# The expert stage computed on sorted tokens instead of on all tokens

## The reference

```
logits = xf @ gate_w.T                                # xf: 2048 x 256, rms-normalised
topk_vals, topk_idx = top_k(logits, 2)
topk_gates = softmax(topk_vals)
gates = zeros((2048, 8)); gates[row, topk_idx] = topk_gates
h = silu(einsum('nd,ehd->neh', xf, exp_w1))           # every expert on every token
eo = einsum('neh,edh->ned', h, exp_w2)
sel = einsum('ned,ne->nd', eo, gates)                 # six of the eight gates of a token are zero
out = x + silu(xf @ sh_w1.T) @ sh_w2.T + sel
```

## Time and profile before

| | |
|---|---|
| time, median of 3 runs | 3418.31 us (3410.98 to 3420.01) |
| profiled execution, first to last instruction | 3419.0 us |
| TensorE matmul busy | 3026.8 us (89%) |
| VectorE, ScalarE, GpSimd busy | 56%, 44%, 13% |
| mean granted TensorE clock | 0.930 |
| DMA, mean over the span | 48 GB/s |
| expert stage, from its first instruction to the first of the next stage | 1457.6 to 2316.4 us |

### The profile page before, as it was taken

One profiled execution on the slowest core, in us unless ns is written; L12 is line 12 of the kernel. 1 busy time (PEld: TensorE's weight loads), 2 busy tenths in 40 slices (PEclk: granted clock), 3 DMA queues, 4 the chain that ended last, 5 costly groups with the idle time before them and its releaser, 6 DMA issues. The chain is left out here.

```text
span 3419.0 us, 47618 instructions
## 1 busy us (share of the span) xinstructions
PE 3026.8 (89%) x17126; PEld 1808.1 (53%) x17248; DVE 1914.5 (56%) x4677; ACT 1492.1 (44%) x2134; POOL 451.8 (13%) x538
## 2 busy tenths in 40 slices
PE   6888888856999999989999999996999999978686
PEld 3444333342444444379898989993444444347353
DVE  4666777654767776443333333334777777734354
ACT  1333444521555555544444444431555555543233
POOL 0111111143211111010000000001122221113112
PEclk7889888976999999989999999997999999998798
DMA  4212121103222222000000000003222222100331
GB/s 116 49 40 57 46 64 46 30 1 70 76 61 82 67 77 60 18 25 26 26 25 26 26 26 26 1 1 69 78 61 87 58 76 58 30 1 1 83 86 49
DMA packets 75113, 162.66 MB, mean 48 GB/s; under 512 B 15401, under 2 KB 21673, under 8 KB 72697
## 3 DMA queue, kind: packets, MB, share of 16 engines
q1 hardware_dynamic: 74872, 159.51, 17.8%
HBM read 60.76 MB, written 2.10 MB: 18 GB/s over the span
## 5 line engine op out<-in xcount | busy, mean ns | idle before, releaser
L883 ACT ACTIVATE probT_a<-scores 128x1024 f32<-128x1024 f32 (+3 forms) x832 | 785.1, 949 | 841.8 <-PE scores L737 469.8
L992 DVE CUSTOM_DVE_ANT_0 ring<-ring,maskb_a 128x512 f32<-128x512 f32 x1024 | 681.9, 719 | 204.8 <-PE ring L754 175.1
L754 PE MATMUL ring<-stacks_a 64*128 64x512 f32 (+7 forms) x1664 | 451.9, 422 | 72.2 <-DMA stacks_a<-fixed_a 26.0
L1329 DVE TENSOR_TENSOR hidden_moe<-whole_moe,hidden_moe 128x512 fp32r<-128x512 f32 x288 | 199.8, 694 | 519.9 <-ACT whole_moe L1251 519.7
L775 PE MATMUL outputs<-probT_a,V_a 128*32 128x512 f32 (+6 forms) x3328 | 451.1, 586 | 23.9 <-ACT probT_a L883 11.8
L1172 PE MATMUL scores<-tokens_moe,weights_moe 128*128 128x512 f32 x1728 | 447.8, 395 | 4.9 <-issue 4.9
L719 PE MATMUL scores<-stacks_a 64*128 64x512 f32 (+7 forms) x1664 | 415.6, 480 | 0.0
L719 PEld LDWEIGHTS scores<-stacks_a 64*128 64x128 f32 (+1 forms) x1664 | 166.4, 188 | 464.0 <-issue 344.9
L990 DVE TENSOR_REDUCE negm_a<-ring 128x1 f32<-128x512 f32 (+3 forms) x640 | 329.7, 562 | 144.5 <-PE ring L760 103.2
L1185 PE MATMUL ring<-weights_moe,hidden_moe 128*128 128x256 f32 x2592 | 402.8, 283 | 4.0 <-DVE hidden_moe L1329 3.4
L1185 PEld LDWEIGHTS ring<-weights_moe,hidden_moe 128*128 128x128 f32 x2592 | 367.6, 191 | 30.7 <-issue 4.6
(11 more groups left out here) (151 smaller groups left out, 3240.7 us busy)
## 6 DMA issues: line engine op xcount, KB each, us to landing
stacks_a<-parts_a SPq DMA_DIRECT2D x672, 128.0 KB
raw<-in_moew SPq DMA_DIRECT2D x9, 2048.0 KB, 7.5
maski_a<-in_mask SPq DMA_DIRECT2D x16, 1024.0 KB, 5.3
wt<-in_w SPq DMA_DIRECT2D x7, 1024.0 KB, 5.0
kvT_a<-in_ctxT SPq DMA_DIRECT2D x12, 512.0 KB, 3.5
stacks_a<-fixed_a SPq DMA_DIRECT2D x4, 1024.0 KB
wrow<-in_row SPq DMA_DIRECT2D x7, 512.0 KB, 6.2
stacks_a<-mrow_a SPq DMA_DIRECT2D x224, 8.0 KB
```

The source lines that it names most:

```text
L754: last = pe.matmul(bank("S", j, n, e)[:, 0:w], Q[rows, g, qt * P:(qt + 1) * P], K[rows, g, 0:w], start=True, stop=not a.causal)
L883: act.activation(probT[:, kb % 2, 2 * p:2 * p + 2, q0:S], scores_bank(j, n)[:, :, q0:S], ACT.Exp, bias=0.0, scale=-1.0).then_inc(c_exp.sem, 1)
L992: least = dve.tensor_tensor_reduce(sc, sc, maskb[:, m % 2, qt, :], 1.0, BIG * 2, ALU.add, ALU.min, out)
L1329: dve.tensor_tensor(hidden[:, m % 4, 1, :], whole[:, m % 2, :], hidden[:, m % 4, 0, :].bitcast(F32), ALU.subtract).then_inc(c_low.sem, 1)
```

## The change

The eight experts are no longer computed on all tokens; the shared one still is. `feed_block` serves f0 and f2 alone; a new `routed_block` lays out the expert stage.

- The beginning of the stage is as before, but the normalised tokens are also stored to a DRAM tensor `moe_tokens`, and four copies of `xs` exist instead of two.
- The shared expert comes first, 32 steps as before. Beside them the routing is worked out: ranks of the (token, expert) pairs within their expert by 17 float32 matmuls with a triangle and with ones (step 6), the extent of each expert in tiles of 256 slots (steps 7 and 8), the slot of each pair, and by 32 float32 matmuls with one-hot matrices (steps 15 to 22) the token and the gate of each slot (`addresses`, step 23).
- Then come 23 tiles of 256 slots, the number that suffices whatever the draw; all 23 are always computed. A tile is 4 steps. A step is 12 matmuls of 256 columns (two slices of the hidden width over 256 slots), the same two Silu of 512 columns, the same subtraction, and 12 matmuls of 256 columns of the second layer.
- Each tile loads its expert's 2 MB in four quarters by SyncE, whose address comes from a value computed on chip; ScalarE and VectorE split one quarter (1024 columns) in each step.
- GpSimd gathers a tile's 2 x 128 rows by two indirect DMAs; TensorE turns them with 4 transposes, ScalarE and VectorE split them. The outputs are scaled by the gate on ScalarE (256 columns, twice) and added by two indirect DMAs with accumulation into a DRAM tensor `moe_total`, each pair after the pair before it has landed.
- After the last tile SyncE reads `moe_total` back in four pieces and VectorE adds them to X.
- At the start of the program GpSimd zeroes `raw`, and SyncE writes it to `moe_total` (2 MB and 256 KB), ahead of the copies into `stacks`.
- The first-layer results use three PSUM banks in turn instead of four; the fourth serves the routing and the turned rows.

```diff
+SL = 2 * P
+TILES = (2 * NT * P + E * (SL - 1)) // SL
...
+                sp.wait_ge(m_zero, 1)
+                sp.dma_start(total[0:NT * P, :].rearrange("(p n) d -> p (n d)", p=P), raw[:, :]).then_inc(m_cleared, 16)
+                sp.dma_start(total[NT * P:(NT + 2) * P, :].rearrange("(p n) d -> p (n d)", p=P), raw[:, 0:2 * D])                    .then_inc(m_cleared, 16)
...
+            for i in range(TILES):
+                e = sp.value_load(expert_i[0:1, i:i + 1], min_val=0, max_val=E)
+                for c in range(4):
+                    sp.wait_ge(m_wlow, 4 * i + c + 1)
+                    sp.dma_start(raw[:, quarter(c)], io["moew"][bass.ds(e, 1), :, quarter(c)]
+                                 .rearrange("o p n -> (o p) n")).then_inc(m_raw[c], 16)
+            sp.wait_ge(m_scatter, 32 * TILES)
+            for b in range(B):
+                sp.dma_start(xs(b), total[b * QT * P:(b + 1) * QT * P, :].rearrange("(q p) d -> p q d", p=P))\
+                    .then_inc(m_sum[b], 16)
...
+            def gather(i):
+                for j in range(2):
+                    pool.indirect_dma_start(
+                        out=gathered(i, j), out_offset=None, in_=spread_rows[:, :],
+                        in_offset=bass.IndirectOffsetOnAxis(ap=row_from[:, 2 * i + j:2 * i + j + 1], axis=0))\
+                        .then_inc(m_gather[i % 2], 16)
+            def scatter(i):
+                pool.wait_ge(m_scaled, i + 1)
+                if i == 0:
+                    pool.wait_ge(m_cleared, 32)
+                else:
+                    pool.wait_ge(m_scatter, 32 * i)
+                for j in range(2):
+                    pool.indirect_dma_start(
+                        out=total[:, :], in_=scaled(i, j), in_offset=None, compute_op=ALU.add,
+                        out_offset=bass.IndirectOffsetOnAxis(ap=row_to[:, 2 * i + j:2 * i + j + 1], axis=0))\
+                        .then_inc(m_scatter, 16)
+            gather(0)
+            gather(1)
+            for i in range(TILES):
+                if i + 2 < TILES:
+                    pool.wait_ge(m_rows, i + 1)
+                    gather(i + 2)
+                if i >= 1:
+                    scatter(i - 1)
+            scatter(TILES - 1)
...
+            for s in range(STEPS + 2):          # TensorE
+                i, q = step(s)
+                if s < STEPS:
+                    first_layer(s)
+                nxt, at = divmod(s - SHARED + 4, 4)
+                if at == ROWS_AT and 0 <= nxt < TILES:
+                    turn_rows(nxt)
+                if s >= 2:
+                    second_layer(s - 2)
+                if s == RANK_AT:
+                    ranks()
+                if INVERSE_AT <= s < INVERSE_AT + 8:
+                    inverses(s - INVERSE_AT)
...
+            for s in range(STEPS):              # ScalarE
+                act.wait_ge(m_hid, s + 1)
+                if s >= 2:
+                    act.wait_ge(m_low, s - 1)
+                for dst in (hidden[:, s % 4, 0, :], whole[:, s % 2, :]):
+                    last = act.activation(dst, RING[s % 3], ACT.Silu)
+                last.then_inc(m_high, 1)
+                nxt, at = divmod(s - SHARED + 4, 4)
+                if 0 <= nxt < TILES:
+                    whigh(nxt, at)
+                    if at == ROWS_AT:
+                        act.wait_ge(m_rows, nxt + 1)
+                        for kb in range(KB):
+                            act.activation(rowsT[:, nxt % 2, 0, kb, :], TURN[:, kb * SL:(kb + 1) * SL], ACT.Identity,
+                                           bias=0.0, scale=norm3[:, kb:kb + 1]).then_inc(m_rowhigh, 1)
+                if at == 2 and 2 <= nxt:
+                    scale_out(nxt - 2)
```

More of the change, by code:

```diff
@@ L1117, in chunk @@
         def chunk(q):
             return slice(q * S, (q + 1) * S)
-        SPLIT = {6 + 3 * q: q for q in range(f.chunks)} if moe else {}
-        def landed(it, more):
-            before = {"f0": 0, "moe": 1, "f2": 1 + FEED["moe"].experts}[st]
-            return it * (16 * PER_TURN) + 16 * (before + more + 1)
-        @block.sync
-        def _(sp):
-            if moe:
-                with sp.Fori(0, TURNS) as it:
-                    for n in range(PER_TURN):
-                        sp.wait_ge(c_wlow.sem, c_wlow.at(st, it, (n + 1) * f.chunks))
-                        load_expert(sp, st, it * PER_TURN + (n + 1))
+        landed = 16 if st == "f0" else 48
@@ L1235, in _ @@
         @block.scalar
         def _(act):
-            def split(it, slot, q, done):
-                if q == 0:
-                    act.wait_ge(c_raw, landed(it, done))
-                act.activation(weights[:, slot, 0, chunk(q)], raw[:, chunk(q)], ACT.Copy).then_inc(c_whigh.sem, 1)
-            def turn(it, experts):
-                for m in range(experts * f.blocks):
-                    slot, n, at = m // f.blocks, m % f.hb, m % f.blocks
-                    act.wait_ge(c_hid.sem, c_hid.at(st, it, m + 1))
-                    act.wait_ge(c_low.sem, c_low.at(st, it, max(m - 1, 0)))
-                    for dst in (hidden[:, m % 4, 0, :], whole[:, m % 2, :]):
-                        if moe:
-                            last = act.activation(dst, RING[m % 4], ACT.Silu)
-                        else:
-                            last = act.activation(dst, RING[m % 4], ACT.Relu, bias=wcolf[:, n:n + 1], scale=1.0)
-                    last.then_inc(c_high.sem, 1)
-                    if experts > 1 and at in SPLIT:
-                        split(it, 1 - slot, SPLIT[at], slot + 1)
@@ L1266, in _ @@
                 b, kb = j // KB, j % KB
[L1267 to L1272 removed]
+                if j == 0:
+                    act.wait_ge(c_raw, landed)
@@ L1282, in _ @@
-            if moe:
-                act.wait_ge(c_gex, 1)
-                act.activation(gex[:, 1, :], gex[:, 0, :], ACT.Exp).then_inc(c_gate, 1)
-                with act.Fori(0, TURNS) as it:
-                    turn(it, PER_TURN)
-                turn(TURNS, 1)
-            else:
-                turn(0, 1)
+                act.activation(tokens[:, 0, kb, b * S:(b + 1) * S], RING[j % 4], ACT.Copy).then_inc(c_thigh.sem, 1)
+            for m in range(f.blocks):
+                n = m % f.hb
+                act.wait_ge(c_hid.sem, c_hid.at(st, 0, m + 1))
+                act.wait_ge(c_low.sem, c_low.at(st, 0, max(m - 1, 0)))
+                for dst in (hidden[:, m % 4, 0, :], whole[:, m % 2, :]):
+                    last = act.activation(dst, RING[m % 4], ACT.Relu, bias=wcolf[:, n:n + 1], scale=1.0)
+                last.then_inc(c_high.sem, 1)
```

758 lines of the change are left out of this document (544 added, 214 removed).

## The result

The changed kernel takes 2997.3 us (median of 4 runs, 2989.05 to 3005.43) against 3418.1 us before: ratio 0.8779 (95% interval 0.8757 to 0.88). The forecast was 2995. (3418.1 is the median of four runs; the table ahead has the first three.) The profiled execution has a span of 2995.0 us against 3419.0.

A forecast was written before the change was run, and what follows sets the result against it. TensorE, bound by columns, was taken to set the pace; the expert stage falls from 859 to 426.5 us (29.5 + 381 + 16), so 3419.0 - 432.5 + 8 = 2994.5, forecast 2995 us, range 2965 to 3085.

The forecast's parts named there:

- TensorE's pace: In the tiles: TensorE bound by columns, 2.86 us a step, 11.9 us a tile with the turned rows; 62% as forecast.
- the turning: In each tile: 4 transposes of the gathered rows on TensorE, 0.5 us a tile, 11.5 us in all.
- Main part: Expert stage between beginning and end: shared expert 90.2, tiles 263.1, turning 11.5, routing 14, fill and drain 2: 381 us.
- the routing matmuls: Beside the shared expert: 17 + 32 float32 matmuls, 98 records on TensorE, 12 to 22 us, taken as 14.
- ScalarE 85%, VectorE 8.5 us a tile: In the tiles: ScalarE 10.1 us, 85% of a tile, and VectorE 8.5 us, both hidden behind TensorE's 11.9.
- 1.5 us an indirect DMA: GpSimd's two gathers and two scatters in each tile: 1.5 us apiece, 6 us a tile, hidden.
- Rival C: In the tiles: GpSimd blocks VectorE's subtractions, a tile 13.1 us, 28 us more, 3023 us; 17% with late weights and slow ScalarE.
- the beginning stays 29.5: Expert stage before its main part: stays 29.5 us, from 1457.6 to 1487.01.
- The row of 1.84 us: Profile row used for rival C: a two-operand SBUF subtraction took 1.84 us beside a GpSimd operation, 0.69 alone.
- The end: After the last second-layer matmul: scaling, scatters, landing, read-back and addition uncovered, 17.4 us, taken as 16; bounds 11 to 28.
- The program start: Before the first stack copy: two issues and 2.25 MB of writes add 8 us, bounds 1 to 12.
- The range of A: Whole kernel if TensorE sets the tiles' pace: 2975 to 3015 us, from routing, start and tail; chance 62%.

The follow-up runs named there:

- the two kernels with the quarter behind the tiles: Changed kernel with the shared expert's last quarter computed after the tiles: alone 2986.6 us; with later clears and 512-column pieces in the beginning too, 2979.2 us.
- the fastest version: Changed kernel with clears moved to the first attention stage, 512-column pieces in the beginning, and the shared expert's last quarter after the tiles: 2979.2 us.

## Why the prediction was right, point by point

- **TensorE's pace.** Steps of 2.87 us (2.86 forecast), the turning 0.44 (0.5), a tile 11.95 (11.9). Two tiles fewer took 23.9 us off TensorE's part; ScalarE's margin was shown by doubling its rounding, GpSimd's by doubling the indirect DMAs, the weights' by undoing the quarters. Main part: 381.3 us (1499.15 to 1880.46) for 381. That it fits to 0.3 us is luck: the routing matmuls were 3.7 + 6.5 = 10.2 us instead of 14 and the turning 1.4 us less in all, and the first blocks at the low clock (18 first-layer matmuls take 6.38 us here, 5.83 in the earlier trace rows), two waits for VectorE's additions (0.90 and 1.62 us) and 0.01 us on each of the steps made up for it.
- **ScalarE 85%, VectorE 8.5 us a tile:** 80% = 9.6 us, and 70% = 8.4 us. ScalarE's margin was larger than priced, mostly by a slip in the sum: the earlier trace rows gave 1.20 - 0.21 = 0.99 us for a Silu pair, and I took 1.1, 0.4 us a tile.
- **GpSimd.** 1.5 us an indirect DMA was the middle: 0.94 for a quiet gather, 1.55 for a scatter, 0.1 to 1.1 us more when held, plus 0.3 between them. A tile occupies the queue for 8.3 us against 6 forecast; hidden both ways.
- **Rival C** asked the right question about the wrong side. In the tiles no subtraction exceeded 1.23 us; it was GpSimd that was held. It did happen in the beginning: the argument "the beginning stays 29.5" overlooked that subtractions of 1024 columns meet GpSimd's normalisation for longer than those of 512. It became 31.4 us (+2.0). The row of 1.84 us was rightly read; what was wrong is the step from it to the tiles, where an indirect DMA is held and doesn't hold.
- **The end:** 17.9 us; my terms added to 17.4 and I had shaved that to 16 because the scatters' halves would overlap. They didn't: 1.55 + 0.3 + 1.55, then the landing. The 17.4 came that near by compensation: the landing took 2.2 us instead of 4, and from the read-back's issue to the next stage 10.9 instead of 9.5.
- **The program start:** +5.1 instead of +8. The writes cost 4.1 us of waiting, not 7: most of the 2.25 MB ran beside loads, slowly.
- **The whole.** The expert stage lost 428.3 us instead of 432.5: beginning 1.9, main part 0.3 and end 1.9 us longer than forecast, 4 in all. The start was 2.9 us cheaper, and the other stages, which the sum left alone, came out 0.6 us shorter in this profile: 1.6 longer to a2 beyond the start, a2 and a3 3.5 longer, a4 to f2 5.2 and a6 0.5 shorter. 2994.5 + 4.0 - 2.9 - 0.6 = 2995.0. So the mechanism and the stage's price to 1% are the forecast's merit, the 0.1% of the whole is luck. The differences outside belong to no step: they lie within what executions of the same code differ by, that from a4 to f2 only if the two kernels with the quarter behind the tiles are counted.
- **The range of A** was added up too narrow: its three terms give 2981 to 3019, not 2975 to 3015. Nothing hung on it.

## What to carry to other kernels

Where one engine is bound by columns and the trace has a start-to-start time per column, a rewritten stage can be priced closely (here a tile at 11.9 us that takes 11.95); spend the remaining effort on the two ends of the stage, where nothing is hidden, and on every duration whose partner engine changes. Indirect DMAs of 128 rows cost their engine 0.9 to 2.5 us each here and are free as long as their sum with the gaps stays under the tile. A weight buffer refilled in pieces as it is consumed needs no second copy; refilled whole it costs the wait and then the clock.

## What was not expected of the hardware

- An indirect DMA on GpSimd is delayed by the remainder of the VectorE instruction that runs when it starts (up to 1.09 us), not by what starts later, and not if it starts within 0.04 us of that instruction (27 cases). VectorE pays nothing, while beside GpSimd's elementwise work it does (2.25 us instead of 1.22).
- A stand of 5.8 us of TensorE took back clock too: twelve matmuls behind it took 2.48 us instead of 1.60, at a granted clock of 0.53 for 5 us.
- 2 MB written to DRAM took 13.0 us among the program's first loads and 6.8 us at 270 us; quarters of weights landed in 4.4 us beside scatters and 3.9 without.
- The same attention code before the second attention stage's constants differed by up to 19 us between executions, which is more than any of the three edits of the fastest version takes off; what makes it differ was not tried.
